# An attention kernel's exchange issued by SyncE in both halves, and its high weights multiplied against both value halves at once

## The chip, the cores and the metric

The kernel runs on one core of one Trainium2 chip. The metric is device time in microseconds (us) of one execution; the kernel before took 712.77 us (median of 3 runs, 710.68 to 718.14).

## What is computed

One layer over 4096 rows of width 256: h = relu(layernorm(x)), attention with a dense 4096 x 4096 matrix added twice to the scores, and a residual.

```python
h = jnp.maximum(_layernorm(x, axis=-1), 0.0)
q = h @ Wq.T + bq
k = h @ Wk.T + bk
v = h @ Wv.T + bv
a = q @ k.T * scale + adj + adj          # 4096 x 4096
x = x + jax.nn.softmax(a, axis=-1) @ v
```

Everything is fp32, and the kernel keeps that accuracy by splitting each fp32 operand of a matmul into two fp16 halves, a high one and a low one, and multiplying three of the four pairs.

## The kernel before

**Tiles and periods.** Output rows come in 32 tiles of 128 rows, two tiles (t = 0 and 1) to a pair p, 16 pairs. The 4096 keys come in 4 quads of 1024. A period n = 4p + q handles quad q of pair p; there are 64. In the steady state (n = 7 to 63) period n makes the scores of its own quad, takes the exponential of unit u = n - 4, and weighs the values with unit n - 7. A unit is one tile and half of the keys: u = 4p + 2 half + t. It has two parts of 1024 keys, and 4 pieces for weighing.

**TensorE (PE).** `period` in the tensor block writes its order out by hand: `product_1`, `product_3` of the period before, a quarter of `weigh`, `product_6`, `product_2`, a quarter, `product_7`, `product_5`, a quarter, `product_4`, the last quarter. Seven products of 3 matmuls of 512 moving columns (L1524) make the scores by a Strassen-like scheme. Each quarter of `weigh` (L1457 is the helper's line) multiplies 4 blocks: w_hi by v_hi, w_hi by v_lo, and after the wait for `split_lo` w_lo by v_hi, each with 256 moving columns, all summed into columns 0 to 255 of one PSUM bank of 512. v_hi and v_lo of a block lie next to each other in `v_sb`.

**VectorE (DVE).** Its order is written out too: `scores_11` (L1089), `finish_12` of the period before (L1111), `scores_12` (L1096), `finish_11`, `turn(u, 0)` (32x32 transposes in place, L1138), `scores_22` (L1104), `finish_22`, `turn(u, 1)`, `finish_21`, and at the end of periods with n mod 4 = 2 and 3 `row_bias` (L1152) and `finish` (L1201), which scales an output tile out of PSUM and adds it to `xy`. PE's `product_6`, `product_7` and `product_4` each wait until DVE has read the bank `t_ps[n % 2]` (`t_read`), by `scores_11`, `scores_12` and `scores_22`.

**The exchange.** A 128 x 1024 part whose 32x32 blocks are turned still lies in the wrong partitions. `exchange_a(u)` on SyncE (L436) moves part 0 of the unit and `exchange_b(u, i)` on ScalarE (L801) part 1, each with 4 DMAs of 128 KB, SBUF to SBUF, from `rows` to `xT`. `xT` has 3 buffers. ScalarE's `high` (L818) then casts a piece to its high fp16 half, GpSimd's `low` (L641) makes the low half. Pieces from number LATE = 233 on (in unit 58) are cast by DVE instead (`late_high`, L1147), among them all 4 of the last unit, 63.

**Refills.** `rows` is a ring of 15 units of 512 KB that the matrix is loaded into. Once a part has left by the exchange, `refill(u, part)` on SyncE (L388) loads the row unit 15 further on; `scores_11` and the others wait for it.

**SyncE's queue (SP)** is in order: a wait holds all behind it. In period n it runs `store` (n mod 4 = 0), `exchange_a(u)`, `load_xy` (L395; waits until the store of the tile 6 back has landed), `load_g` (L416), `refill(u - 1, 0)`, `refill(u - 1, 1)`, `store` (n mod 4 = 3; L401, waits for `finish`).

Of the kernel before, what the change touches and what calls it, by code (L numbers as in the profile page):

```python
# [9 lines left out]
ALU = mybir.AluOpType  # L10
# [3 lines left out]
P = 128  # L14
N = 4096
D = 256
# [6 lines left out]
QUADS = 4  # L23
# [22 lines left out]
SETUP = 7  # L46
LATE = 4 * (PERIODS - WEIGH_LAG) + 5
LAST_UNITS = 3
B11, B21, B22, T3, T1, T2, T4 = range(7)
A11, A12, A21, A22, S1, S2, S3, S4 = range(8)  # L50

# [18 lines left out]
def attention_kernel(nc, x, adj, wq, bq, wk, bk, wv, bv, out):  # L70
# [4 lines left out]
    with ctx:  # L75
# [3 lines left out]
        def sem(name):  # L79
            return ctx.enter_context(nc.semaphore(name))  # L80
# [157 lines left out]
        weighed = sem("weighed")  # L238
        sum_step = sem("sum_step")
        y_done = sem("y_done")  # L240

        def wait(eng, s, value):

# [133 lines left out]
        def _(sp):  # L377
# [41 lines left out]
            def move_v(g):  # L419

                first = g // HALF_CHUNKS * BLOCKS
                k = g % HALF_CHUNKS
                group = slice(k // 2 * 2 * Q + k % 2, (k // 2 + 1) * 2 * Q, 2)
                sp.wait_ge(v_lo_done, 2 * g + 2)
                for i in range(P // Q):
                    sp.dma_start(v_sb[group, first + i:first + i + 13:4].rearrange("p t s d -> p t (s d)"),  # L426
                                 vn[g % 2][i * Q:(i + 1) * Q].rearrange("p u t s d -> p (u t) (s d)")
                                 ).then_inc(v_moved[g % 2], 16)

            def exchange_a(u):  # L430
# [4 lines left out]
                for i in range(P // Q):  # L435
                    sp.dma_start(arrivals(u)[0:2 * Q, i].rearrange("p j q -> p (j q)"),  # L436
                                 row[i * Q:(i + 1) * Q, :]).then_inc(landing(u, 0), 16)

            def refill(u, part):

                p, half, t = unit_parts(u)
                r = 2 * (QUADS * p + 2 * half + part) + t + ROW_UNITS
                if r < 2 * PERIODS:
                    sp.wait_ge((moved_b if part else moved_a)[u % XT], 64 * (u // XT + 1))
                    load_rows(r)
# [53 lines left out]
            load_rows(13)  # L499
            exchange_a(0)  # L500
            store_g(4)
            refill(0, 0)
            store_g(5)
            move_v(6)
            move_v(7)
            sp.wait_ge(v_moved[0], 64 * (GROUPS // 2))
            load_rows(14)
            store_g(6)
            store_g(7)
            refill(0, 1)  # L510
            exchange_a(1)
            exchange_a(2)
            refill(1, 0)
            refill(1, 1)

            def period(n):
                p, u = n // QUADS, n - EXP_LAG
                if n % QUADS == 0 and p >= 3:
                    store(2 * (p - 3) + 1)
                if unit_in_range(u):  # L520
                    exchange_a(u)
                if n % QUADS in (0, 1) and 2 <= p < PAIRS:
                    load_xy(2 * p + n % QUADS)
                if n % QUADS == 0 and p + 1 < PAIRS:
                    load_g(p + 1)
                if unit_in_range(u - 1):
                    refill(u - 1, 0)
                if unit_in_range(u - 1):
                    refill(u - 1, 1)
                if n % QUADS == 3 and p >= 2:  # L530
                    store(2 * (p - 2))

            for n in range(SETUP, PERIODS + WEIGH_LAG + 2):
                period(n)
# [183 lines left out]
        def _(act):  # L718
# [227 lines left out]
            evict_g(4, 0)  # L946
            high_v(12)
            high_query(2)
            exchange_b(0, 0)
            evict_g(4, 1)  # L950
            evict_g(5, 0)
            exchange_b(0, 1)
            high_v(13)
            exponential(1, 0)
            exponential(1, 1)
            high_v(14)
            scale_adj(4)
            evict_g(5, 1)
            exchange_b(0, 2)
            exponential(2, 0)  # L960
            high_v(15)
            evict_g(6, 0)
            exchange_b(0, 3)
            exponential(2, 1)
            evict_g(6, 1)
            evict_g(7, 0)
# [1 line left out]
            high(0)  # L968
            scale_adj(5)
            high(1)  # L970
            exchange_b(1, 0)
            scale_adj(6)
            exchange_b(1, 1)
            exchange_b(1, 2)
            exchange_b(1, 3)

            def period(n):
                p, u = n // QUADS, n - EXP_LAG
                m = 4 * (n - WEIGH_LAG)
                if n % QUADS == 0:  # L980
                    exchange_b(u - 1, 0)
                    high(m + 2)
                    exchange_b(u - 1, 1)
                    high(m + 3)
                    exponential(u, 0)
                    exchange_b(u - 1, 2)
                else:
                    exponential(u, 0)
                    exchange_b(u - 1, 0)
                    high(m + 2)  # L990
                    exchange_b(u - 1, 1)
                    high(m + 3)
                    exchange_b(u - 1, 2)
                scale_adj(n)
                exchange_b(u - 1, 3)
# [16 lines left out]
            exchange_b(u - 1, 0)  # L1012
            high(LATE - 3)
            exchange_b(u - 1, 1)
            high(LATE - 2)
            high(LATE - 1)
            exponential(u, 0)
            exchange_b(u - 1, 2)
            exponential(u, 1)
            exchange_b(u - 1, 3)  # L1020
            exponential(u + 1, 0)
            exchange_b(u, 0)
            exponential(u + 1, 1)
# [18 lines left out]
        def _(dve):  # L1042
# [139 lines left out]
            def sums(tile):  # L1182
# [9 lines left out]
                nc.vector.tensor_tensor(out_scale[:, one], inv_sum[:, one], inv_omega[:], ALU.mult  # L1192
                                        ).then_inc(sum_step, 1)

            def finish(tile):
                t = tile % 2
                y = xy[:, tile % XY, :]
# [180 lines left out]
            def period(n):  # L1378
                p, u = n // QUADS, n - EXP_LAG
                scoring = n < PERIODS  # L1380
                if scoring:
                    scores_11(n)
                if SETUP < n <= PERIODS:
                    finish_12(n - 1)
                if n % QUADS == 0 and 1 <= p <= PAIRS:
                    bias(2 * p - 2)
                if scoring:
                    scores_12(n)
                    finish_11(n)
                if n % QUADS == 0 and 1 <= p <= PAIRS:  # L1390
                    bias(2 * p - 1)
                turn(u, 0)
                if scoring:
                    scores_22(n)
                    finish_22(n)
                turn(u, 1)
                if scoring:
                    finish_21(n)
                if n % QUADS in (2, 3) and p < PAIRS:
                    row_bias(2 * p + n % QUADS - 2)  # L1400
                if n % QUADS == 0 and p >= 2:
                    sums(2 * p - 4)
                if n % QUADS == 1 and p >= 2:
                    sums(2 * p - 3)
                if n % QUADS == 2 and p >= 2:
                    finish(2 * p - 4)
                if n % QUADS == 3 and p >= 2:
                    finish(2 * p - 3)

            for n in range(SETUP, PERIODS):  # L1410
                period(n)
# [26 lines left out]
            sums(TILES - 3)  # L1438
            late_high(LATE + 13)
            late_high(LATE + 14)  # L1440
            finish(TILES - 4)
            for m in range(LATE + 15, LATE + 17):
                late_high(m)
            finish(TILES - 3)
# [5 lines left out]
            sums(TILES - 1)  # L1450
            finish(TILES - 2)
            finish(TILES - 1)

        @block.tensor
        def _(pe):
# [113 lines left out]
            def weigh(u, part):  # L1569
# [16 lines left out]
                for k in range(KT):  # L1586
                    block = 4 * part + k
                    kt = half * BLOCKS + block
                    w_hi = piece(m)[:, k, 0]
                    matmul(out_bank(2 * p + t)[:, 0:D], w_hi, v_sb[:, kt, 0], half == 0 and block == 0, False)  # L1590
                    matmul(out_bank(2 * p + t)[:, 0:D], w_hi, v_sb[:, kt, 1], False, False)
# [186 lines left out]
```

## Time and profile before

| | |
|---|---|
| median of 3 runs | 712.77 us |
| lowest, highest | 710.68, 718.14 us |
| the profiled execution | 712.38 us |
| its span, first to last instruction | 710.6 us |
| PE busy | 689.6 us, 97% |
| DVE busy | 581.3 us, 82% |
| ACT busy | 431.6 us, 61% |
| POOL busy | 427.6 us, 60% |
| DMA queue q1 (SP) | 126.39 MB, 69.7% of 16 engines |
| DMA queue q10 (ACT) | 33.70 MB, 20.1% |

Busy shares of PE are of modelled ends, since matmuls overlap; the start-to-start distance of groups in the timeline is the better measure, and it is used below. "SPq" and "ACTq" rows are the issuing of DMAs.

### The profile page before, as it was taken

The page shows a single profiled execution, that of the slowest core. Times are in us where ns is not written, and L with a number is a line of the kernel's source. Part 1 is how long each engine was busy: PE and PEld are TensorE (multiplying, and loading weights), DVE is VectorE, ACT ScalarE, POOL GpSimd, SP SyncE. Part 2 cuts the span into 40 slices and gives each one's busy share as a digit, 9 for nine tenths or more (in the row PEclk, how much of TensorE's full clock was granted, in tenths as well). Part 3 has the DMA queues.
Part 4 walks back from the last instruction along what each step waited for, and adds up shares of the span by engine and source line. Part 5 has one row for each costly group of instructions (what it writes and reads, how often), then busy time and mean ns, then how long its engine had stood idle before and what let it go on. Part 6 is the DMA issues. An engine that isn't in the chain of part 4 may idle for free.

```text
span 710.6 us, 14184 instructions
## 1 busy us (share of the span) xinstructions
PE 689.6 (97%) x4799; PEld 475.1 (67%) x4799; DVE 581.3 (82%) x1284; ACT 431.6 (61%) x732; POOL 427.6 (60%) x434
## 2 busy tenths in 40 slices
PE   5789999999999999999999999999999999999998
PEld 4556546676666666766766676667666667666786
DVE  4899788888888888788888888797877878887897
ACT  4899564756755675657576565746566665656440
POOL 1879506564754665665657474656637575655587
PEclk9999999999999999999999999999999999999999
DMA  8558699999999999999989898989998899988572
GB/s 267 172 161 263 169 249 302 267 234 245 216 225 240 242 250 203 261 224 266 232 239 236 215 249 237 249 229 234 211 253 222 243 230 228 249 234 211 127 208 68
DMA packets 85048, 160.99 MB, mean 227 GB/s; under 512 B 12784, under 2 KB 33648, under 8 KB 84976
## 3 DMA queue, kind: packets, MB, share of 16 engines
q1 hardware_dynamic: 64336, 126.39, 69.7%
q10 hardware_dynamic: 20640, 33.70, 20.1%
q8 instruction: 38, 0.62, 0.4%
q14 instruction: 34, 0.28, 0.1%
HBM read 80.35 MB, written 8.39 MB: 125 GB/s over the span
## 4 chain that ended last, share of the span: by engine, by line
PE 74%; DMA 13%; ACT 3%; SPq 3%; DVE 2%; issue 2%; POOL 1%; ACTq 1%; DVEq 0%; POOLq 0%
PE bank L1457 42%; PE bank L1524 32%; DMA xT<-rows 4%; DMA out_y<-xy 3%; DMA rows<-in_adj 3%; ACT rows L723 1%; DMA xy<-in_x 1%; PE bank L1471 1%; DMA rows<-in_x 1%; DMA g_scratch<-xT 1%; SPq L436 1%; SPq L426 1%; SPq L407 1%; ACTq L801 1%; DMA v_sb<-rows 1%
## 5 line engine op out<-in xcount | busy, mean ns | idle before, releaser
L641 POOL TENSOR_TENSOR wT<-xT,wT 128x512 f16<-128x512 f32 x233 | 267.4, 1163 | 191.0 <-ACT wT L818 190.9
L1457 PE MATMUL bank<-v_sb,wT 128*128 128x256 f16 x2796 | 342.6, 273 | 0.0
L1524 PE MATMUL bank<-top,a_op 128*128 128x512 f16 x1344 | 331.1, 379 | 3.3 <-DVE rows L1089 1.4
L1457 PEld LDWEIGHTS bank<-v_sb,wT 128*128 128x128 f16 x2796 | 273.6, 98 | 80.5
L818 ACT CAST wT<-xT 128x512 f16<-128x512 f32 x233 | 139.1, 611 | 141.8 <-DVE rows L1138 129.3
L1524 PEld LDWEIGHTS bank<-top,a_op 128*128 128x128 f16 x1344 | 130.8, 98 | 112.7 <-DVE rows L1096 3.1
L1111 DVE CUSTOM_DVE_ANT_0 rows<-bank,rows 128x512 f32<-128x512 f32 x256 | 173.7, 680 | 12.1 <-PE bank L1524 3.4
L792 ACT ACTIVATE rows<-rows,exp_bias,exp_scale 128x1024 f32<-128x1024 f32 x128 | 158.3, 1237 | 35.8 <-DVE exp_bias L1178 29.1
L1138 DVE STREAM_TRANSPOSE rows<-rows 128x1024 f32<-128x1024 f32 x128 | 158.4, 1239 | 0.2 <-ACT rows L792 0.2
L1096 DVE SCALAR_TENSOR_TENSOR rows<-rows,adj_scale,bank 128x512 f32<-128x512 f32 x64 | 47.8, 746 | 53.5 <-PE bank L1524 53.5
L1089 DVE SCALAR_TENSOR_TENSOR rows<-rows,adj_scale,bank 128x512 f32<-128x512 f32 x64 | 47.6, 744 | 27.8 <-PE bank L1524 20.9
L1104 DVE SCALAR_TENSOR_TENSOR rows<-rows,adj_scale,bank 128x512 f32<-128x512 f32 x64 | 47.2, 737 | 6.9 <-PE bank L1524 6.9
L783 ACT ACTIVATE rows<-rows,adj_scale 128x512 f32<-128x512 f32 x64 | 45.9, 718 | 4.4 <-POOL wT L641 1.3
L823 ACT ACTIVATE h_tile<-xy,ln_all 128x256 f32<-128x256 f32 x32 | 19.2, 601 | 42.0 <-DMA xy<-in_x 41.9
L618 POOL TENSOR_TENSOR a_op<-g_pair,a_op 128x512 f16<-128x512 f32 x15 | 17.4, 1162 | 31.3 <-ACT a_op L777 31.3
L1457 PE MATMUL bank<-v_sb,top 128*128 128x256 f16 x276 | 30.3, 273 | 0.0
L1457 PEld LDWEIGHTS bank<-v_sb,top 128*128 128x128 f16 x276 | 26.4, 98 | 3.7
L792 ACT ACTIVATION_READ_ACCUMULATOR rows<-rows,exp_bias,exp_scale 128x1 f32 x128 | 23.9, 187 | 0.0
L1152 DVE CUSTOM_DVE_ANT_0 h_tile<-h_tile,wqbk_row,rbias 128x256 f32<-128x256 f32 x32 | 23.7, 739 | 0.0
L648 POOL TENSOR_TENSOR xy<-xy,bv_row 128x256 f32<-128x256 f32 x32 | 23.6, 736 | 0.0
L608 POOL TENSOR_TENSOR comb<-g_pair 128x128 f32<-128x128 f32 x15 | 6.9, 458 | 26.2 <-DMA g_pair<-g_scratch 26.2
L1457 PE MATMUL bank<-xT,top 128*128 128x256 f16 x144 | 20.2, 280 | 2.5 <-DVE rows L1079 2.3
(115 smaller groups left out, 452.7 us busy)
## 6 DMA issues: line engine op xcount, KB each, us to landing
rows<-in_adj SPq DMA_DIRECT2D x128, 512.0 KB, 8.1
xT<-rows SPq DMA_DIRECT2D x244, 128.0 KB, 4.2
xT<-rows ACTq DMA_DIRECT2D x244, 128.0 KB, 6.5
rows<-in_x SPq DMA_DIRECT2D x8, 512.0 KB, 6.0
xy<-in_x SPq DMA_DIRECT2D x32, 128.0 KB, 4.8
g_scratch<-xT SPq DMA_DIRECT2D x16, 256.0 KB, 4.6
g_pair<-g_scratch SPq DMA_DIRECT2D x15, 256.0 KB, 5.0
out_y<-xy SPq DMA_DIRECT2D x30, 128.0 KB, 7.9
```

The costliest lines, as they stand in the source:

```text
L641: nc.gpsimd.tensor_tensor(split_piece(m, 1), exchanged(m), split_piece(m, 0), ALU.subtract).then_inc(split_lo, 1)
L783: nc.scalar.activation(part, part, ACT.Copy, scale=adj_scale[:]).then_inc(adj_scaled, 1)
L792: nc.scalar.activation(row, row, ACT.Exp, scale=exp_scale[:], bias=exp_bias[:, p % 2, t:t + 1], accum_out=unit_sum(u, part)).then_inc(expe ...
L818: nc.scalar.copy(split_piece(m, 0), exchanged(m)).then_inc(split_hi, 1)
L1089: nc.vector.scalar_tensor_tensor(part, part, adj_scale[:], t_ps[n % 2][:], ALU.mult, ALU.add).then_inc(t_read[n % 2], 1)
L1096: nc.vector.scalar_tensor_tensor(part, part, adj_scale[:], t_ps[n % 2][:], ALU.mult, ALU.add).then_inc(t_read[n % 2], 1)
L1104: nc.vector.scalar_tensor_tensor(part, part, adj_scale[:], t_ps[n % 2][:], ALU.mult, ALU.add).then_inc(t_read[n % 2], 1)
L1111: return nc.vector.tensor_tensor_reduce(out=row, in0=ps[:], in1=row, scale=1.0, scalar=-3.0e38, op0=ALU.add, op1=ALU.max, accum_out=chunk_ ...
L1138: nc.vector.transpose(unit_row(u, part), unit_row(u, part)).then_inc(turned, 1)
L1152: nc.vector.tensor_tensor_reduce(out=h, in0=h, in1=wqbk_row[:], scale=SCORE_SCALE / H_SCALE, scalar=rbias0[:], op0=ALU.mult, op1=ALU.add, ...
L1457: return nc.tensor.matmul(out_ap, stationary, moving, start=first, stop=last)
L1524: last = nc.tensor.matmul(ps[:], s, mv, start=first and k == 0, stop=k == 2, skip_group_check=True)
```

## The change

1. **SyncE issues both halves.** A new `exchange_b(u)` on SyncE issues the 4 DMAs of part 1. ScalarE keeps them for the last four units only.
2. **SyncE's order in a period** becomes: `store` (n mod 4 = 0), `store` (n mod 4 = 3), `exchange_a(u)`, `refill(u - 1, 1)`, `load_xy`, `load_g`, `exchange_b(u)`, `refill(u, 0)`. The set-up's order changes likewise.
3. **Weighing.** For tiles 0 to 30 the two matmuls w_hi v_hi and w_hi v_lo become one of 512 moving columns: the first lands in columns 0 to 255 of the bank, the second in 256 to 511. Tile 31 stays as it was.
4. **VectorE** adds the second half with a new `add_low`, once per tile for tiles 0 to 30, and both `add_low` and `finish` move from the end of the period to before and behind `turn(u, 0)`.

```diff
             def period(n):                       # SyncE
                 if n % QUADS == 0 and p >= 3:
                     store(2 * (p - 3) + 1)
+                if n % QUADS == 3 and p >= 2:
+                    store(2 * (p - 2))
                 if unit_in_range(u):
                     exchange_a(u)
+                if unit_in_range(u - 1):
+                    refill(u - 1, 1)
...
-                if unit_in_range(u - 1):
-                    refill(u - 1, 0)
-                if unit_in_range(u - 1):
-                    refill(u - 1, 1)
-                if n % QUADS == 3 and p >= 2:
-                    store(2 * (p - 2))
+                if unit_in_range(u) and n < PERIODS:
+                    exchange_b(u)
+                if unit_in_range(u):
+                    refill(u, 0)
...
             exchange_a(1)                        # SyncE, set-up
+            exchange_b(1)
             exchange_a(2)
             refill(1, 0)
+            exchange_b(2)
             refill(1, 1)
+            refill(2, 0)
...
+            def add_low(tile):                   # VectorE
+                if tile >= WIDE_TILES:
+                    return
...
+                nc.vector.scalar_tensor_tensor(y, out_bank(tile)[:, D:2 * D], out_scale[:, t:t + 1], y,
+                                               ALU.mult, ALU.add).then_inc(low_added, 1)
...
+                done = 2 * p - 6 + n % QUADS
+                if n % QUADS >= 2 and p >= 2:
+                    add_low(done)
                 turn(u, 0)
+                if n % QUADS >= 2 and p >= 2:
+                    finish(done)
...
+            add_low(TILES - 4)                   # VectorE, the last units
             finish(TILES - 4)
...
+                    if 2 * p + t < WIDE_TILES:   # PE, weigh
+                        matmul(out_bank(2 * p + t)[:], w_hi, v_sb[:, kt].rearrange("p s d -> p (s d)"), first, False)
+                    else:
+                        matmul(out_bank(2 * p + t)[:, 0:D], w_hi, v_sb[:, kt, 0], first, False)
+                        matmul(out_bank(2 * p + t)[:, 0:D], w_hi, v_sb[:, kt, 1], False, False)
```

## Rows read from the trace of the kernel before

**Rows 1.** The page: PE's busy time, and its granted clock and DMA's share by slice.
```profile
PE 689.6 (97%) x4799; PEld 475.1 (67%) x4799; DVE 581.3 (82%) x1284; ACT 431.6 (61%) x732; POOL 427.6 (60%) x434
...
PEclk9999999999999999999999999999999999999999
DMA  8558699999999999999989898989998899988572
```

**Rows 2.** Timeline of PE, 104 to 114 us: start, length, line, operation, count.
```profile
104.28 7.93 PE L1524 MATMUL bank<-top,a_op 128*128 128x512 f16 x36
112.05 1.47 PE L1457 MATMUL bank<-v_sb,wT 128*128 128x256 f16 x12
113.36 0.81 PE L1524 MATMUL bank<-top,a_op 128*128 128x512 f16 x3
```

**Rows 3.** Timeline of PE around its three stalls after 104 us.
```profile
121.82 1.47 PE L1457 MATMUL bank<-v_sb,wT 128*128 128x256 f16 x12
123.60 1.47 PE L1524 MATMUL bank<-top,a_op 128*128 128x512 f16 x6 [0.31 <-DVE rows L1089]
...
220.03 1.47 PE L1457 MATMUL bank<-v_sb,wT 128*128 128x256 f16 x12
221.62 1.47 PE L1524 MATMUL bank<-top,a_op 128*128 128x512 f16 x6
...
533.03 1.47 PE L1457 MATMUL bank<-v_sb,wT 128*128 128x256 f16 x12
535.62 1.47 PE L1524 MATMUL bank<-top,a_op 128*128 128x512 f16 x6 [1.11 <-DVE rows L1089]
```

**Rows 4.** The chain of waits ahead of the stall at 535.62 us: start, length, what.
```profile
514.81 9.85 DMA out_y<-xy
...
525.83 8.96 DMA rows<-in_adj
```

**Rows 5.** Timeline of all engines, 340 to 348 us (a period with n mod 4 = 2).
```profile
341.02 1.24 DVE L1138 STREAM_TRANSPOSE rows<-rows 128x1024 f32<-128x1024 f32 x1
...
342.42 0.75 DVE L1104 SCALAR_TENSOR_TENSOR rows<-rows,adj_scale,bank 128x512 f32<-128x512 f32 x1 [0.16 <-PE bank L1524]
...
344.11 0.81 PE L1524 MATMUL bank<-top,a_op 128*128 128x512 f16 x3
...
345.68 1.26 DVE L1152 CUSTOM_DVE_ANT_0 h_tile<-h_tile,wqbk_row,rbias 128x256 f32<-128x256 f32 x1
...
346.87 0.47 DVE L1201 SCALAR_TENSOR_TENSOR xy<-bank,out_scale,xy 128x256 f32<-128x256 f32 x1
347.27 0.73 DVE L1089 SCALAR_TENSOR_TENSOR rows<-rows,adj_scale,bank 128x512 f32<-128x512 f32 x1
```

**Rows 6.** Timeline of SP's queue, 318 to 362 us, one period.
```profile
342.29 2.48 SPq L436 DMA_DIRECT2D xT<-rows  x4
344.81 1.06 SPq L388 DMA_DIRECT2D rows<-in_adj  x2
```

**Rows 7.** The page's DMA issues: count, KB each, median us from issue to landing.
```profile
rows<-in_adj SPq DMA_DIRECT2D x128, 512.0 KB, 8.1
xT<-rows ACTq DMA_DIRECT2D x244, 128.0 KB, 6.5
```

**Rows 8.** The line of exchange_a (L436) by itself: its landings.
```profile
DMA to landing us min/median/max: 2.6/4.2/9.2
```

**Rows 9.** Timeline of all engines, 690 to 711 us, the tail.
```profile
690.94 15.51 POOL L641 TENSOR_TENSOR top<-rows,top 128x512 f16<-128x512 f32 x12 [0.36 <-DVE top L1147]
...
693.79 0.47 DVE L1201 SCALAR_TENSOR_TENSOR xy<-bank,out_scale,xy 128x256 f32<-128x256 f32 x1
...
694.29 14.17 SPq L401 DMA_DIRECT2D out_y<-xy  x4
...
700.01 4.31 DVE L1147 CAST top<-rows 128x512 f16<-128x512 f32 x4
...
707.44 0.48 DVE L1201 SCALAR_TENSOR_TENSOR xy<-bank,out_scale,xy 128x256 f32<-128x256 f32 x1 [1.70 <-issue]
```

More of the change, by code:

```diff
@@ L48 @@
 LAST_UNITS = 3
+WIDE_TILES = TILES - 1
 B11, B21, B22, T3, T1, T2, T4 = range(7)
@@ L240, in attention_kernel @@
         y_done = sem("y_done")
+        low_added = sem("low_added")
         def wait(eng, s, value):
@@ L437, in exchange_a, with exchange_b @@
                                  row[i * Q:(i + 1) * Q, :]).then_inc(landing(u, 0), 16)
+            def exchange_b(u):
+                sp.wait_ge(turned, 2 * u + 2)
+                arrival_free(sp, u)
+                for i in range(P // Q):
+                    sp.dma_start(arrivals(u)[2 * Q:P, i].rearrange("p j q -> p (j q)"),
+                                 unit_row(u, 1)[i * Q:(i + 1) * Q, :]).then_inc(landing(u, 1), 16)
             def refill(u, part):
@@ L501, in _ @@
             store_g(4)
+            exchange_b(0)
             refill(0, 0)
+            move_v(6)
             store_g(5)
-            move_v(6)
             move_v(7)
+            store_g(6)
             sp.wait_ge(v_moved[0], 64 * (GROUPS // 2))
             load_rows(14)
-            store_g(6)
             store_g(7)
@@ L948, in _ @@
             high_query(2)
-            exchange_b(0, 0)
             evict_g(4, 1)
             evict_g(5, 0)
-            exchange_b(0, 1)
             high_v(13)
@@ L958, in _ @@
             evict_g(5, 1)
-            exchange_b(0, 2)
             exponential(2, 0)
@@ L962, in _ @@
             evict_g(6, 0)
-            exchange_b(0, 3)
             exponential(2, 1)
@@ L970, in _ @@
             high(1)
-            exchange_b(1, 0)
             scale_adj(6)
-            exchange_b(1, 1)
-            exchange_b(1, 2)
-            exchange_b(1, 3)
             def period(n):
@@ L979, in period @@
                 m = 4 * (n - WEIGH_LAG)
+                if n % QUADS:
+                    exponential(u, 0)
+                high(m + 2)
+                high(m + 3)
                 if n % QUADS == 0:
[L981 to L984, printed above, removed]
                     exponential(u, 0)
[L986 to L993, printed above, removed]
                 scale_adj(n)
-                exchange_b(u - 1, 3)
                 exponential(u, 1)
@@ L1011, in _ @@
             u = PERIODS - EXP_LAG
-            exchange_b(u - 1, 0)
             high(LATE - 3)
-            exchange_b(u - 1, 1)
             high(LATE - 2)
@@ L1017, in _ @@
             exponential(u, 0)
-            exchange_b(u - 1, 2)
             exponential(u, 1)
-            exchange_b(u - 1, 3)
             exponential(u + 1, 0)
@@ L1193, in sums @@
                                         ).then_inc(sum_step, 1)
+            def add_low(tile):
+                if tile >= WIDE_TILES:
+                    return
+                t = tile % 2
+                y = xy[:, tile % XY, :]
+                dve.wait_ge(sum_step, 3 * tile + 3)
+                dve.wait_ge(weighed, 4 * (tile_units(tile) + 1))
+                dve.wait_ge(xb_done, tile + 1)
+                nc.vector.scalar_tensor_tensor(y, out_bank(tile)[:, D:2 * D], out_scale[:, t:t + 1], y,
+                                               ALU.mult, ALU.add).then_inc(low_added, 1)
             def finish(tile):
                 t = tile % 2
+                if tile < WIDE_TILES:
+                    dve.wait_ge(low_added, tile + 1)
                 y = xy[:, tile % XY, :]
@@ L1404, in period @@
                     sums(2 * p - 3)
[L1405 to L1408, printed above, removed]
             for n in range(SETUP, PERIODS):
@@ L1443, in _ @@
                 late_high(m)
+            add_low(TILES - 3)
             finish(TILES - 3)
@@ L1450, in _ @@
             sums(TILES - 1)
+            add_low(TILES - 2)
             finish(TILES - 2)
@@ L1589, in weigh @@
                     w_hi = piece(m)[:, k, 0]
-                    matmul(out_bank(2 * p + t)[:, 0:D], w_hi, v_sb[:, kt, 0], half == 0 and block == 0, False)
-                    matmul(out_bank(2 * p + t)[:, 0:D], w_hi, v_sb[:, kt, 1], False, False)
+                    first = half == 0 and block == 0
+                    if 2 * p + t < WIDE_TILES:
[3 more added lines that the diff above has]
+                        matmul(out_bank(2 * p + t)[:, 0:D], w_hi, v_sb[:, kt, 1], False, False)
                 pe.wait_ge(split_lo, m + 1)
```

## The prediction

> **What bounds the kernel now.** First the page: PE is 97% busy and its granted clock is 1.0 in every slice, the 2.4 GHz level [rows 1]; VectorE follows at 82%. A busy share of PE is no proof, since its matmuls overlap, so I went to the timeline of PE and took distances between the starts of groups. 36 matmuls of 512 columns take 112.05 - 104.28 = 7.77 us, 215.8 ns each; 12 of 256 columns take 113.36 - 112.05 = 1.31 us, 109.2 ns each [rows 2]. 512 columns at 2.4 GHz are 213.3 ns and 256 are 106.7, so a matmul costs its columns and 2.5 ns. One period has 21 of the first and 48 of the second: 4.53 + 5.24 = 9.77 us. I compared each start with this sum: from 104 us to the last matmul PE falls behind it at three places only. There the 12 matmuls (1.31 us) are followed after 1.78, 1.59 and 2.59 us: stalls of 0.47, 0.28 and 1.28 us, 2.03 in all [rows 3]. So PE's stream of columns bounds the kernel for 600 us, and no other engine can give more than these 2.03 us there.
>
> The chain of waits says where the stalls are from: the one at 535.62 goes back from DVE's L1089 to a refill of `rows` that landed after 8.96 us, and that was issued behind a `load_xy` which held SP until an output store had landed, 9.85 us [rows 4]. The matrix came late because SP's queue stood behind a store.
>
> **The change, step by step.**
>
> *Wide weighing.* 31 tiles x 2 units x 16 blocks = 992 pairs become one matmul each. A pair costs 2 x 109.2 = 218.4 ns, one of 512 costs 215.8: 2.6 ns less, 992 x 2.6 = 2.6 us. The columns are the same, only a fixed cost per instruction goes. The loads of weights that fall away overlapped with matmuls. This is on the path: -2.6 us. From below it is 0 (if both forms cost their columns alone), from above nothing more is in the rows.
>
> *add_low on VectorE.* 31 more instructions of the form of `finish`. That is 0.47 us long, and the next begins 347.27 - 346.87 = 0.40 us after its start [rows 5]: 31 x 0.40 = 12.4 us of DVE. What matters is its place. In the period shown, `turn(u, 0)` starts at 341.02 and is 1.24 us long, `scores_22` started at 342.42 after waiting 0.16 us for PE, and PE needs its result for `product_4` at 344.11 [rows 5]. With both additions and the turn at its full length: turn at 341.42, `finish` at 342.66, `scores_22` at 343.06, done 0.75 later at 343.81. That is 0.30 us ahead of 344.11; I take 0.05 of it for the signal: hidden, with 0.25 us of cover. Without the cover each 0.1 us costs 31 x 0.1 = 3.1 us. `finish_22` and the second turn start later than before by 0.6 us at most, but `finish` (0.40) and the wait of 0.16 are gone, so `scores_11` of the next period is not late. `bias` falls into periods without the additions.
>
> *SP's order.* The exchange, 4 DMAs, takes SP 2.48 us, two refills 1.06 [rows 6]. The new period costs SP 2 x 2.48 + 1.06, at most 1.6 for store, `load_xy` and `load_g`: 7.6 of 9.77 us, so SP keeps up. What its queue now waits for: `exchange_b(u)` for the second turn; `refill(u, 0)` for the landing of `exchange_a(u)`. Behind that stands the next `exchange_a`, 9.77 us after the last: 2.48 of issue and 4.2 of landing fit in, a landing over about 7 us would hold it. For the unit whose exchange starts at 342.29 the first refill went out a period later, at 344.81 + 9.77 = 354.6 [rows 6]; now it waits for the landing only, 342.29 + 3 x 0.62 + 4.2 = 348.4 [rows 6, 8], 6 us sooner, behind no store and ahead of the next `load_xy`. That is 12 us into period n, and the row unit is read from period n + 3 on, 29 us into it: 17 us for a transfer that takes 8.1 [rows 7]. I take the stalls at 221 and 535 us as gone: -1.56. The set-up's stall at 121 us is different: there eight exchange issues come ahead of `refill(1, 0)` and now twelve, but store and moves of v come earlier. Bounds 0.47 less and 1 more; I take -0.2.
>
> The transfers of part 1 lose their own queue. The trace has them landing in 6.5 us on ACT's, against 4.2 for SP's [rows 7, 8], and the data is wanted more than a period after landing, so a few us more cost nothing: 0. On this the Trainium skill (DMA: Bandwidth & Descriptors, Queues, rings and completion order) says that each engine takes turns between queue rows, so on SP's row part 1 must stand behind the 512 KB loads where it had turns of its own; by that rule the step would be a loss where the exchange is near its deadline.
>
> *ScalarE* loses 4 issues a period and the wait for the turn. It was 61% busy [rows 1] and no stall of PE names it: 0.
>
> *The tail.* In SP's new order `store(28)` comes ahead of `exchange_a(63)`, whose data the last 4 casts of DVE need. `finish(28)` starts at 693.79 and SP's store goes out at 694.29; the casts start at 700.01, back to back with what is before them, and GpSimd's last 12 subtractions run without a gap from 690.94 to 706.45, just ahead of PE's last matmuls, after which `finish(31)` starts at 707.44 [rows 9]. New: `add_low(28)` pushes `finish(28)` by 0.40 and its store to 694.7; 0.6 for its issue and 3 x 0.6 for three more, so the last part of the exchange is issued at 697.1 and lands, at 4.2 us [rows 8], at 701.3. `add_low(28)` and `(29)` alone would bring the casts to 700.8. So the casts start 1.3 us late, GpSimd ends 1.0 to 1.3 us late, and it was about 0.3 ahead (706.45, 4 matmuls of 0.11 and the read-out, against 707.44): +0.8 us at the end. Bounds: 0.4 (the additions alone), and 5.5 for a landing of 9.2 us [rows 8].
>
> **Sum.** -2.6 - 1.56 - 0.2 + 0.8 = -3.6 us on a span of 710.6, which lay in an execution of 712.38: 708.8. The median shown is 0.4 above that execution, so 709.2 us.
>
> **Rivals.**
> 1. *DVE takes the cover of 0.25 us.* If an addition is stretched to what `row_bias` took in this very period on a tile of the same shape, 1.26 us instead of 0.47 [rows 5], `product_4` stalls by 0.79 - 0.25 = 0.54 us in 31 periods: +17 us, 726 us. For it: DVE is the second engine, and the additions stand right ahead of a read that PE waits for. Against: the `finish` behind that `row_bias` took 0.47. It decides from where `scores_22` ends after 344.11 on this period's clock. This is the slower side. In part (0.2 us each) it gives 715.
> 2. *SP becomes the bound of the exchange or of the refills.* If issues slow down to 0.9 us when the queues are full (DMA's share is 9 in nearly all slices [rows 1]), a period costs SP 8 x 0.9 + 2.7 = 9.9 us, over 9.77: 57 x 0.1 = 6 us more, and the old stalls stay: 715. The rule of the skill above points the same way.
> 3. *The tail eats the gain:* landing at 9.2 us, +5.5 instead of +0.8: 713.9; half of it 711.5.
> 4. *The wide form gains nothing,* since the bank is written over its full width and cost follows columns alone: 709.2 + 2.6 = 711.8.
> 5. *Wide matmuls are far cheaper than in [rows 2].* A sustained 512-column stream well under 213 ns would give tens of us. 36 of them in a row at 215.8 ns speak against it. The Trainium skill (TensorE: Matmul & The Clock Gate, Back-to-back issue gap) gives a sustained 131 ns at N = 512; by that figure 992 x 87 ns = 86 us would go, which is an estimate from the page and disagrees with the 215.8 ns here.
>
> **Chances.** Forecast 0.63, rival 1 0.08, rival 2 0.10, rival 3 0.10, rival 4 0.08, rival 5 0.01. The forecast itself spans 707 to 711: the runs before lay within 710.68 to 718.14, and the stalls differ from run to run. The range 706.5 to 714.5 takes in the forecast, rivals 3 and 4 and about half of rival 2 and leaves out some 0.15. One per cent, about what a measurement of this kernel can tell from no change, is 7.1 us: faster needs under 705.6, which is more than all stalls after 104 us and the wide form together (4.6) and would have to come from the set-up or rival 5: 0.05. Slower needs over 719.9: rival 1 in full, and the far end of rival 2: 0.08. The rest, 0.87, is within 1%.
>
> **What would show it.** PE's groups: 4 matmuls of 512 and 4 of 256 a quarter, 1.300 us from start to start instead of 1.310, and a period of 9.73 instead of 9.77 us. `scores_22` in periods with n mod 4 = 2 and 3 without a wait for PE, ending some 0.3 us ahead of `product_4`. No wait of L1089 for rows<-in_adj after 200 us. In the tail the last four casts about 1 us later than the end of the scores makes them now. The prediction is wrong if PE shows idle ahead of L1524 with a DVE line as releaser every fourth period, or if the wide matmuls' distance is not 215.8 ns, or if SP's exchange slips later from period to period.

## The result, and the profile after

The changed kernel took 775.1 us (median of 4 runs, 763.1 to 787.6) against 712.9 us before: a ratio of 1.072, 95% interval 1.061 to 1.083. The forecast was 709.2 us, within 1%. It is slower by 7%: wrong in sign, and the 51 us that the ratio stands for are some twenty times the largest term of the sum. The ratio goes by the executions of each kernel within 1.5% of its fastest, here 763.1 and 766.6 us; the profiled one took 783.6 us (its span is 781.8), so the trace shows some 20 us more of the same loss than the ratio does.

The page of the changed kernel, its busy times, its slices, and the lines of its longest chain:

```profile
PE 709.8 (91%) x3807; PEld 381.8 (49%) x3807; DVE 601.7 (77%) x1315; ACT 417.8 (53%) x732; POOL 426.3 (55%) x434
...
PEclk9999999899998999999999999999999999989999
DMA  8467999999999999999999999999999999999773
...
DMA packets 85039, 160.85 MB, mean 206 GB/s; under 512 B 12784, under 2 KB 33648, under 8 KB 84976
...
DMA 49%; PE 23%; SPq 13%; issue 5%; POOL 4%; ACT 3%; DVE 2%; ACTq 0%; POOLq 0%; DVEq 0%
```

Beside [rows 1], PE went from 97 to 91%, and no other engine took its place: DVE, ACT and POOL all have more idle time as well. The chain is made of transfers and of SyncE's queue. The bytes are those of before, moved at 206 GB/s on the mean against 227.

Where PE lost its time shows in the same reckoning as before, each group's start against the sum of its columns. After 104 us PE of the kernel before fell behind at 3 places by 2.0 us [rows 3]; now at 50 places by 73.2. At 30 of them, 57.3 us, the profile names what ended a wait; at 20, 15.9 us, there is no wait. The difference, 71.2 us, is as large as that of the spans (781.8 - 710.6), though the wide matmuls should have given 2.6 us back; some 3 us of the tally stay unassigned. The timeline of PE of the changed kernel:

```profile
295.41 1.03 PE L1469 MATMUL bank<-v_sb,wT 128*128 128x512 f16 x4
299.27 0.61 PE L1469 MATMUL bank<-v_sb,wT 128*128 128x256 f16 x4 [2.83 <-POOL wT L657]
299.71 2.48 PE L1536 MATMUL bank<-top,a_op 128*128 128x512 f16 x6
301.98 2.18 PE L1469 MATMUL bank<-v_sb,wT 128*128 128x512 f16 x8
...
328.00 1.46 PE L1536 MATMUL bank<-top,a_op 128*128 128x512 f16 x6
329.30 1.46 PE L1469 MATMUL bank<-v_sb,wT 128*128 128x512 f16 x8
```

Undisturbed, 6 matmuls of 512 columns take 329.30 - 328.00 = 1.30 us. After the stall for GpSimd's low halves the same 6 take 301.98 - 299.71 = 2.27: a part ran at the 1.2 GHz level, and the granted clock of 299.5 to 302 us is 0.60. So a late piece can cost PE twice, once by waiting and once by the clock, which was granted at 0.973 on the mean. It does not always: after a stall of 2.48 us at 342.54 the next 6 took 1.29 us.

GpSimd's casts were late because the exchange was, or because `g_pair` was, which SyncE issues behind the same waits. The waits of the changed kernel, all engines and then SyncE's queue (total us, times, longest):

```profile
ACT h_tile L839 <- DMA xy<-in_x: 196.4, 28, 9.4
...
POOL comb L624 <- DMA g_pair<-g_scratch: 111.5, 14, 9.4
...
PE bank L1469 <- POOL wT L657: 40.9, 22, 3.0
...
SPq L390 <- DMA xT<-rows: 228.9, 109, 4.5
```

The last line is the finding: SyncE stands at its refills for the landing of the exchange 109 times, 228.9 us in all; before it was 42.1 us in 20 times. Of the 109, 54 are at `refill(u - 1, 1)`, 132.7 us, and 55 at `refill(u, 0)`, 96.1 us. What this does to the period is in the chain of waits of the changed kernel (start, length, what):

```profile
339.97 0.54 SPq L446
...
341.84 6.65 DMA xT<-rows
348.49 0.02 issue
348.51 0.52 SPq L390
...
349.13 0.54 SPq L446
...
351.00 8.42 DMA xT<-rows
359.42 0.02 issue
359.44 0.33 SPq L390
359.77 0.04 issue
359.82 0.43 SPq L397
...
360.36 10.10 DMA g_pair<-g_scratch
```

L446 is `exchange_b`, L390 a refill, L397 `load_xy`. Read it as a circle: `exchange_b(u)` is issued (1.87 us from its first issue to its last), lands, the landing frees `refill(u, 1)`, and behind that refill in the same queue stands `exchange_b(u + 1)`. No engine that computes is in it. One turn takes 1.87 + landing + 0.45 us (0.64 in the first turn shown), and about 1 more with `load_xy` and `load_g`. PE needs a turn in 9.73 us, so the last of the four DMAs may take 7.4 us to land, or 6.5 with both loads. Here it took 6.65 and 8.42: the turns are 349.13 - 339.97 = 9.16 us and, with the loads, 360.82 - 349.13 = 11.69. From 160 to 640 us the last of the four took 8.2 us to land on the mean, and `exchange_a` is issued every 11.02 us, where it was every 9.79. `exchange_a(u)`, its landing, `refill(u, 0)` and `exchange_a(u + 1)` make a second circle of the same length.

### The profile page after: what moved, and what is told of

Read it like the earlier page. It is cut to its first block, busy times and chain, and to the rows that moved or that the text cites. A ratio compares the mean times of both kernels' runs of the same rounds, so it can differ in the third digit from the quotient of the medians.

```text
span 781.8 us, 12107 instructions
## 1 busy us (share of the span) xinstructions
PE 709.8 (91%) x3807; PEld 381.8 (49%) x3807; DVE 601.7 (77%) x1315; ACT 417.8 (53%) x732; POOL 426.3 (55%) x434
## 4 chain that ended last, share of the span: by engine, by line
DMA 49%; PE 23%; SPq 13%; issue 5%; POOL 4%; ACT 3%; DVE 2%; ACTq 0%; POOLq 0%; DVEq 0%
DMA xT<-rows 42%; PE bank L1469 14%; SPq L446 10%; PE bank L1536 8%; DMA g_pair<-g_scratch 6%; POOL wT L657 2%; SPq L390 2%; SPq L397 1%; ACT rows L739 1%; PE bank L1483 1%; DMA g_scratch<-xT 1%; DMA rows<-in_x 1%; DVE rows L1133 0%; POOL a_op L634 0%; ACT top L765 0%
## 5 line engine op out<-in xcount | busy, mean ns | idle before, releaser
L1469 PE MATMUL bank<-v_sb,wT 128*128 128x256 f16 (+1 forms) x1864 | 351.8, 331 | 51.2 <-POOL wT L657 40.9
L1536 PE MATMUL bank<-top,a_op 128*128 128x512 f16 x1344 | 342.3, 389 | 3.4 <-DVE rows L1084 1.6
L1469 PEld LDWEIGHTS bank<-v_sb,wT 128*128 128x128 f16 x1864 | 182.8, 99 | 234.3 <-POOL wT L657 52.0
L1536 PEld LDWEIGHTS bank<-top,a_op 128*128 128x128 f16 x1344 | 133.7, 100 | 118.5 <-issue 10.6
L834 ACT CAST wT<-xT 128x512 f16<-128x512 f32 x233 | 133.9, 611 | 42.8 <-issue 25.3
L1084 DVE SCALAR_TENSOR_TENSOR rows<-rows,adj_scale,bank 128x512 f32<-128x512 f32 x64 | 47.6, 744 | 28.7 <-PE bank L1536 26.0
L1469 PE MATMUL bank<-v_sb,top 128*128 128x256 f16 (+1 forms) x216 | 30.1, 302 | 0.0
L1469 PEld LDWEIGHTS bank<-v_sb,top 128*128 128x128 f16 x216 | 21.1, 98 | 8.8
```

The lines of the kernel that those rows point to most:

```text
L834: nc.scalar.copy(split_piece(m, 0), exchanged(m)).then_inc(split_hi, 1)
L1084: nc.vector.scalar_tensor_tensor(part, part, adj_scale[:], t_ps[n % 2][:], ALU.mult, ALU.add).then_inc(t_read[n % 2], 1)
L1469: return nc.tensor.matmul(out_ap, stationary, moving, start=first, stop=last)
L1536: last = nc.tensor.matmul(ps[:], s, mv, start=first and k == 0, stop=k == 2, skip_group_check=True)
```

## The experiments

Ratios are to the kernel before, timed beside each, with 95% intervals. "Pitch" is the mean distance of two `exchange_a` between 160 and 640 us of the profiled execution; landings are medians of single DMAs, so somewhat under what SyncE waits for, the last of four. An empty cell was not read. Kernels written as "after, but" are the changed kernel with one edit.

| kernel | ratio | pitch, us | lands: `exchange_a`, `exchange_b`, matrix |
|---|---|---|---|
| after | 1.072 (1.061 to 1.083) | 11.02 | 6.2, 6.4, 7.8 |
| e1_wide_only | 0.999 (0.996 to 1.002) | | |
| e2_sp_only | 1.043 (1.036 to 1.049) | 10.37 | 5.4, 5.7, 7.4 |
| e3_b_on_act | 1.013 (1.005 to 1.020) | 10.13 | 4.9, 6.2, 7.5 |
| e4_refills_last | 1.004 (1.000 to 1.008) | 9.71 | 4.1, 4.0, 6.2 |
| e5_small_first | 1.094 (1.086 to 1.101) | 11.27 | 5.3, 6.5, 7.9 |
| e6_loop_cut_small_late | 1.006 (1.002 to 1.010) | 9.85 | 4.0, 3.6, 6.4 |
| e7_small_first_refills_last | 0.994 (0.991 to 0.997) | 9.72 | 4.5, 4.2, 6.2 |
| e8_finish_back | 1.085 (1.079 to 1.092) | 10.98 | |
| e9_wide_no_add | 1.077 (1.069 to 1.085) | 10.90 | 5.9, 5.9, 7.8 |
| e10_narrow_with_add | 1.051 (1.042 to 1.060) | 10.67 | 5.7, 5.9, 7.6 |
| e11_mended | 0.993 (0.990 to 0.997) | 9.66 | 5.1, 4.7, 6.6 |
| e12_wait_alone | 1.000 (0.995 to 1.005) | 9.86 | 5.4, 5.2, 7.2 |
| f1_refill_ahead_no_wait | 1.090 (1.085 to 1.096) | 11.06 | 5.5, 7.8, 8.5 |
| f2_half_refills | 0.990 (0.984 to 0.996) | 9.72 | 2.8, 3.4, 3.9 |
| f3_mended_narrow | 0.996 (0.993 to 0.999) | | |
| f4_same_place_no_waits | 1.074 (1.066 to 1.083) | 10.54 | 4.4, 6.3, 8.3 |
| h1_late_refills_last | 1.005 (1.001 to 1.009) | 9.95 | 3.6, 3.5, 6.4 |
| h2_refill_ahead_of_a | 1.146 (1.140 to 1.152) | 11.73 | 4.8, 4.9, 5.4 |

**Which part of the change.** e1 takes SyncE's and ScalarE's code from before and keeps the wide weighing; e2 keeps SyncE's new code and takes the weighing and VectorE's order from before; e3 is after, but with part 1 issued by ScalarE, as before.

> Only the wide weighing, add_low and the place of finish; SyncE and ScalarE as before. Theory (the queue of SyncE is the whole loss): PE's quarters start 1.300 us apart instead of 1.310, 992 x 2.6 ns = 2.6 us less on before, the stalls of before stay, ratio 0.996 to 1.000. Rival (VectorE's additions or the wide form cost PE): slower than before by more than 1%, with VectorE lines as releasers of L1536.

> Only the exchange on SyncE with its new order, and ScalarE without it; weighing and VectorE as before. Theory (SyncE's queue): it takes the whole loss, 1.07 like the changed kernel, up to 0.004 more. Rival (the wide weighing or VectorE has a part, for one by letting the clock fall): 1.00 to 1.04.

> The changed kernel, but part 1 of the exchange goes out from ScalarE as before; SyncE keeps its new order of stores, refills and loads. If the loss comes from exchange_b in SyncE's queue (its wait and its DMAs), this is faster than before by 2.6 us (wide) and up to 2 us (stalls): ratio 0.994 to 0.998. If the new order of refills and stores is at fault, it stays at 1.03 to 1.07.

The wide weighing alone is harmless, so SyncE's part is guilty: 4.3% alone, less than the 7 that I expected of it. With part 1 back on ScalarE, 1.3% (0.5 to 2.0) is left of the 7.2, between the two outcomes that I had written down. There `refill(u - 1, 1)` still waits for the landing of `exchange_b`, but what stands behind it is no longer the next `exchange_b`.

**Which of SyncE's steps.** e4 moves one refill:

```diff
                 if unit_in_range(u):
                     exchange_a(u)
-                if unit_in_range(u - 1):
-                    refill(u - 1, 1)
...
                 if unit_in_range(u) and n < PERIODS:
                     exchange_b(u)
+                if unit_in_range(u - 1):
+                    refill(u - 1, 1)
                 if unit_in_range(u):
                     refill(u, 0)
```

e5 leaves the refill and puts `load_xy` and `load_g` ahead of `exchange_a(u)`. e6 puts `exchange_b(u)` ahead of `refill(u - 1, 1)`, and the small loads behind that. e7 is e4 and e5 together.

> The changed kernel, but refill(u - 1, 1) goes out behind exchange_b(u), ahead of refill(u, 0), so that no landing of exchange_b(u - 1) stands ahead of exchange_b(u). Theory A (the loop exchange_b, its landing, refill, next exchange_b, at 10.5 us a period, sets the pace): the loss goes for the most part, ratio under 1.02. Theory B (all DMAs in one queue land late, whatever the waits): 1.04 to 1.08, and xy and g_pair land in 8 to 9 us as in the changed kernel.

> The changed kernel, but SyncE issues load_xy and load_g at the head of the period, ahead of exchange_a(u) and refill(u - 1, 1); the loop exchange_b(u - 1), landing, refill(u - 1, 1), exchange_b(u) stays. Theory A (that loop sets the pace): still 1.04 to 1.07. Theory C (the small loads go out behind a wait and land behind a 512 KB refill, so ScalarE waits for xy and GpSimd for g_pair, and their casts come late to PE): ratio under 1.01, ScalarE's wait for xy falls from 196 us to under 60.

> The changed kernel with the order exchange_a(u), exchange_b(u), refill(u - 1, 1), load_xy, load_g, refill(u, 0): the loop is cut, and the small loads go out still later, behind the second turn and behind a refill. Theory A (loop): under 1.015. Theory C (small loads late): 1.05 to 1.12, waits for xy and g_pair as long as in the changed kernel or longer.

> The changed kernel with both cures: load_xy and load_g at the head, then exchange_a(u), exchange_b(u), refill(u - 1, 1), refill(u, 0). Both theories: at or under before, 0.994 to 1.000, with no stall behind GpSimd's low half after 200 us.

The place of one refill is worth the whole 7%. That the late small loads (196 and 111 us of waits above) were the cause, which I held for likely, fell with e5: ScalarE's wait for `xy` went from 196 to 66 us and the kernel became slower still, and in e6 ScalarE waits 148 us for `xy` at 1.006. These long waits do not carry the 7%. They are not free either: once the refills are last, the small loads at the head are worth 1% more (e7 at 0.994 against e4 at 1.004). SyncE's issues in e4:

```profile
331.37 0.59 SPq L397 DMA_DIRECT2D xy<-in_x  x1
332.07 0.39 SPq L418 DMA_DIRECT2D g_pair<-g_scratch  x1
332.56 2.48 SPq L446 DMA_DIRECT2D xT<-rows  x4
335.09 1.09 SPq L390 DMA_DIRECT2D rows<-in_adj  x2
336.70 2.48 SPq L438 DMA_DIRECT2D xT<-rows  x4
```

Here both refills go out back to back, since what they wait for has landed, and the next exchange follows at once.

**The weighing and VectorE inside the slower kernel.** e8 is after, but `add_low` and `finish` stand at the end of DVE's period again. e9 leaves `add_low` out, so that the product w_hi v_lo is not added. e10 has the narrow matmuls and still runs `add_low`, which adds a half of the bank that nothing has written.

> The changed kernel, but add_low and finish stand at the end of VectorE's period, where finish was. If their place delays the turns and so SyncE's loop (0.4 and 0.6 us in two of four periods), this gives 1.043 to 1.055, the loss of the exchange alone being 1.043. If the place has no part, 1.065 to 1.08.

> The changed kernel with the wide matmuls but without add_low, so the product of the high weights with the low half of v is left out of the result. The exchange alone gave 1.043, the changed kernel 1.072. If VectorE's added work makes the loop worse: 1.035 to 1.05. If the wide matmuls do: 1.06 to 1.09.

> The changed kernel with the two matmuls of 256 columns as before, and add_low kept, which adds a half of the bank that no weighing fills here, so the result has a wrong term. If VectorE's added work makes the loop worse: 1.06 to 1.09. If the wide matmuls do: 1.035 to 1.05.

DVE's order and its additions have no part in the loss that shows: with the order put back (e8) or the additions left out (e9) the kernel is no faster, and e8, at 1.085, lies a little above the 1.08 that I had written down for it. The matmuls' form has one: narrow 1.043 and 1.051, wide 1.072, 1.077 and 1.085, though wide costs nothing where the queue is sound (e1; e11 against f3 below). What PE falls behind by is 38 us in e2 and 51 in e10 (executions of 748 and 761 us) against 73 and 69 in after and e9 (784 and 781 us). Why the form of the matmuls makes a lengthened circle worse stays open.

**The wait, the bytes, the place.** In e12, which is e4 otherwise, SyncE waits for the landing of `exchange_b(u - 1)` ahead of `exchange_b(u)`, so that the circle of the changed kernel is closed again, but with no refill in it (the diff is against e4):

```diff
+                if unit_in_range(u - 1) and unit_in_range(u) and n < PERIODS:
+                    sp.wait_ge(moved_b[(u - 1) % XT], 64 * ((u - 1) // XT + 1))
                 if unit_in_range(u) and n < PERIODS:
                     exchange_b(u)
                 if unit_in_range(u - 1):
                     refill(u - 1, 1)
```

f1 has `refill(u - 2, 1)` in the place of `refill(u - 1, 1)`, whose data landed long ago: the bytes stay, that wait goes (and with it the set-up's `refill(1, 1)`). f2 is after, but each refill loads only half of its bytes, so that half of the scores use old data and the result is wrong.

> e4 (refills last, ratio 1.004) with nothing but a wait added: exchange_b(u) waits until exchange_b(u - 1) has landed; the refill itself stays behind. If the wait in the loop is the price: 1.03 to 1.07. If it is the 512 KB refill that stands ahead of exchange_b in the DMA queue: 1.00 to 1.01.

> The changed kernel with refill(u - 2, 1) where refill(u - 1, 1) stood: a 512 KB refill still goes out directly ahead of exchange_b(u), but the part it waits for landed a period ago, so SyncE waits for nothing there. The wait alone (e12) gave 1.000. If the place of the refill in the DMA queue is the price by itself: 1.03 to 1.07. If it takes both, the wait and the transfer behind it (a loop whose length is a landing under load): 1.00 to 1.02.

> The changed kernel, order and waits untouched, but every refill loads the first half of its row unit only (256 KB instead of 512), so the scores of the other half are made from old data. If the loop is as long as the landing under load: exchange landings fall to 4 to 5 us, the loop is under 9.77 us and PE is the bound again, 0.99 to 1.01. If the in-order waits cost by themselves: 1.04 to 1.07.

The wait alone is free: SyncE stood only 15.5 us at it. With the last of four landing after 6.9 us on the mean (160 to 640 us), where a circle without a refill leaves 9.73 - 1.87 = 7.9 less what little stands between, the circle binds seldom. Half the bytes cure it too: 3.9 us for the last of `exchange_b`'s four. f1 was a miss for me: without that wait it is slower than after. Its chain shows the other circle, `exchange_a(u)`, landing, `refill(u, 0)`, `exchange_a(u + 1)`:

```profile
319.30 0.44 SPq L438
...
321.08 10.59 DMA xT<-rows
331.69 0.33 SPq L390
...
332.12 0.54 SPq L438
```

12.8 us for a turn, with 512 KB of refill going out right behind `exchange_a(u)`, now without delay.

f4 has neither wait in its period: `refill(u - 2, 1)` between the halves and `refill(u - 1, 0)` at the end. h1 has the same two refills, both behind `exchange_b(u)`. h2 is after, but `refill(u - 1, 1)` stands ahead of `exchange_a(u)`.

> f1 still stood 204 us at refill(u, 0), waiting for exchange_a(u) of the same period with a refill beside it. Here both refills keep their places in the queue (one ahead of exchange_b, one behind) but are those of parts that landed a period before: exchange_a(u), refill(u - 2, 1), loads, exchange_b(u), refill(u - 1, 0). If it takes a wait on a landing under load: 0.99 to 1.01, with small waits of SyncE for xT<-rows; landings may be as long as in the changed kernel. If the places in the DMA queue are enough by themselves: 1.04 to 1.09.

> The refills of f4_same_place_no_waits, as late as there (part 1 two periods on, part 0 one period on) and with as few waits for landings, but both behind exchange_b(u) instead of one between the two halves. f4 took 1.074 of the time before, in part since the matrix came late to DVE (63 us of waits for rows<-in_adj) and its loads took 8.3 us to land. Theory D (the place between the halves is what makes landings long): ratio under 1.015, loads of the matrix land in under 7 us, DVE's waits for them under 15 us. Rival E (f4 was slow because its refills came a period later, wherever they stand): ratio 1.04 to 1.08, DVE's waits for rows<-in_adj 40 us or more.

> The changed kernel with one edit: refill(u - 1, 1) stands ahead of exchange_a(u) instead of right behind it, so both halves of the exchange follow one another, while SyncE still stands for the landing of exchange_b(u - 1) in each period and exchange_a(u) has 512 KB ahead of it. Theory F (what hurts is a refill that parts the two halves): ratio under 1.02. Theory G (what hurts is any refill whose wait for a landing stands ahead of the next exchange, and whose 512 KB go right ahead of it): ratio 1.05 or more, exchange_a lands in over 6 us and SyncE's waits for xT<-rows are over 170 us.

f4 against h1 is the cleanest pair: same lateness, same bytes, one line moved, 1.074 against 1.005. f4's SyncE waits 2 us for landings in all, so the circles on SyncE are not the only way to lose, and it did not come out at the 0.99 to 1.01 that I expected if a wait on a landing were needed. The rows of f4 that answer, its waits and then its issues (KB each, median us to landing), and the issues of h1:

```profile
DVE rows L1082 <- DMA rows<-in_adj: 63.4, 21, 7.2
...
rows<-in_adj SPq DMA_DIRECT2D x128, 512.0 KB, 8.3
xT<-rows SPq DMA_DIRECT2D x484, 128.0 KB, 5.5
```

```profile
rows<-in_adj SPq DMA_DIRECT2D x128, 512.0 KB, 6.4
xT<-rows SPq DMA_DIRECT2D x484, 128.0 KB, 3.6
```

With the refill between the halves the exchange lands in 5.5 us and the matrix in 8.3, in the chain of 290 to 340 us up to 11.95; behind both halves it is 3.6 and 6.4. So the place itself lengthens the landings, with no wait to help it. DVE then waits 63 us for the matrix (33 in h1, more than the 15 that I expected there), and the scores, the turn and the next exchange come late with it. This is another path than that of after, where DVE waits 2.6 us for the matrix. What the pair and e4 show is that the place of the refill costs the 7%; that the circles carry it in after is read from its trace, and no run takes its waits away at the same lateness of the refills.

h2, by far the slowest, answers the other question: a refill that parts the two halves is not the only one that hurts. Its exchange lands sooner than after's (4.8 us, not over 6 as I had expected), its refills too (5.4), and its DMA engines are less busy (0.85 of 300 to 600 us against 1.01). Its chain:

```profile
300.43 0.76 SPq L446
...
302.51 5.30 DMA xT<-rows
307.83 0.33 SPq L390
...
308.27 0.55 SPq L438
...
311.13 0.54 SPq L446
...
313.06 4.50 DMA xT<-rows
317.58 0.33 SPq L390
```

Here both halves are issued inside the circle: 1.9 + 0.4 + 2.5 = 4.9 us are fixed (5.4 in the first turn shown), and the landing may take 4.9 us, or 3.5 with both loads. It took 5.3, 4.5 and 6.1, turns of 10.70, 9.47 and 12.40 us. The same sum, with the landing of the last of four as its mean from 160 to 640 us, tells the variants apart: after may take 7.4 to 6.5 and lands in 8.2, f1 (`exchange_a`) 7.4 and 8.2, h2 4.9 to 3.5 and 6.3, all slower; e4 (`exchange_a`) may take 7.4 and lands in 5.3, e11 in 6.3, e12 in 7.1, none slower beyond 0.4%.

What sets the landing is not the refill directly ahead alone. e11 issues `exchange_a` 0.9 us after the start of a refill at the median, h2 0.4 us after it, and single DMAs land in 5.1 and 4.8 us. What orders most runs better is all that had been issued and had not landed when `exchange_a` went out, counted in the traces from 160 to 640 us: 1.28 MB on the mean in e4, 1.36 in before and in e11, 1.47 in e12, 1.63 in f1, 1.74 in after, with 5.3, 5.4, 6.3, 7.1, 8.2 and 8.2 us for the last of four. h2 falls outside this order (1.11 MB and 6.3 us). As an estimate, 1.74 MB at the 209 GB/s of that stretch of after are 8.3 us. No run varies this amount by itself, so it stays a reading of the traces.

**A version that keeps the gain.** e11 is after with SyncE's order mended: `store`, the small loads, `exchange_a(u)`, the even `store`, `exchange_b(u)`, `refill(u - 1, 1)`, `refill(u, 0)`, and the set-up's exchanges and order of before, with `exchange_b(2)` and `refill(2, 0)` at their end. f3 is e11 without the wide weighing.

> The small loads at the head and the refills last, as in e7, and besides the set-up's exchange and order as before (part 1 of units 0 and 1 from ScalarE) and the store of an even tile behind exchange_a. Expected: the stall after 121 us, 3.6 us in e7, is 0.5 again, so 0.988 to 0.994 of before. If the set-up's stall has another cause, 0.993 as e7.

> e11 without the wide weighing and without add_low: the exchange on SyncE in the mended order alone. e11 gave 0.993. The wide weighing is 2.6 us by PE's distances, 0.36%, so this gives 0.995 to 1.000; under 0.993 would mean that the wide form gives nothing even where PE is the bound.

e11 took 710.8 us (707.9 to 714.3, 10 runs) where the kernel before took 715.7 beside it, 0.993 (0.990 to 0.997). That is 0.7% less than before, clear of the noise. Its span is 707.7 us, and PE falls behind at one place after 104 us, by 1.9 us ahead of 124.69 us, so the set-up's stall was not 0.5 again as I had expected. f3's 0.996 leaves 0.3% to the wide weighing, as 2.6 of 710 us would, though the intervals of e11 and f3 overlap.

## Why the prediction was wrong, by its own steps

*Wide weighing, -2.6 us: right where PE is the bound, not in this kernel.* 1.30 us for a quarter of 6 or 8 matmuls, as forecast (the 8 are 4 of 512 and 4 of 256); e11 against f3 is 0.3%, within the noise of the two. In the order of the change the wide form came with more loss, not less (1.072 against 1.043 in e2), which no step foresaw. The Trainium skill (TensorE: Matmul & The Clock Gate, Back-to-back issue gap) has both N / 2.4 GHz + 2.5 ns, which it calls the isolated gap, and the sustained 131 ns of rival 5; this sustained stream, 1.30 us for 6 matmuls of 512, goes by the first.

*add_low hidden: right.* DVE of the changed kernel:

```profile
330.13 0.48 DVE L1198 SCALAR_TENSOR_TENSOR xy<-bank,out_scale,xy 128x256 f32<-128x256 f32 x1
330.52 1.23 DVE L1133 STREAM_TRANSPOSE rows<-rows 128x1024 f32<-128x1024 f32 x1
331.68 0.44 DVE L1209 SCALAR_TENSOR_TENSOR xy<-bank,out_scale,xy 128x256 f32<-128x256 f32 x1
332.04 0.73 DVE L1099 SCALAR_TENSOR_TENSOR rows<-rows,adj_scale,bank 128x512 f32<-128x512 f32 x1
```

`scores_22` follows without a gap and ends at 332.77, and `product_4` starts on time at 333.19: a cover of 0.4 us where 0.30 was worked out. In the page, L1536 waits for DVE's L1084 for 1.6 us in all; rival 1 did not happen.

*The old stalls, -1.56 us: right in itself.* No stall of PE after 200 us goes back to a refill behind a store, and e11 has none left after 125 us. *The set-up's stall, -0.2 us: wrong sign.* It grew from 0.47 to 1.7 us (121.42 to 124.46 us in the changed kernel, for a quarter of 1.30), beyond the bound of 1 more.

*SP's order: here it broke, in one number.* The step had the right limit, "a landing over about 7 us would hold it"; the circle above gives 7.4 to 6.5. It then set the landing at 4.2 us. The changed kernel's was 8.2 us, and this is the term that failed. 4.2 is the median of single DMAs in [rows 8], while SyncE waits for the last of four, which took 5.4 us on the mean already in before; and it was read in the old order, where refills went out behind the exchange. The new order puts 512 KB right ahead of each half on the one queue. At the 240 GB/s that the kernel moves in mid-run (300 to 400 us of before), 512 KB are 2.2 us, and `load_xy` and `load_g`, 384 KB, are 1.6 more. As an estimate made afterwards, 5.4 + 2.2 = 7.6, and 9.2 with them: over 7.4 and 6.5. Such a sum would have been a warning and no more, since bytes directly ahead don't add like this in e11 and h2. The upper row, 9.2 us in [rows 8], was used for the tail only. It also looked at only one of the waits, `refill(u, 0)` for `exchange_a(u)`; that of `refill(u - 1, 1)` for `exchange_b(u - 1)`, which closes the circle of the chain, isn't named in it.

*"SP keeps up" (7.6 of 9.77 us of issue): true and no help.* The issues mostly stayed at 2.48 us for four. A queue in order is bound by issue plus what it stands for.

*Part 1's queue at 0: wrong, though not for turns of queues alone.* The argument was that its data is wanted a period after landing. What wants the landing sooner is the refill behind it. The Trainium skill (DMA: Bandwidth & Descriptors, Queues, rings and completion order) has each engine take turns between queue rows; e3, with the same order on SyncE and part 1 on ScalarE's row, loses 1.3% instead of 7.2, which is the direction of that rule, though e3 also takes `exchange_b` out of SyncE's circle. And e4 and e11 keep part 1 on SyncE's row at 1.004 and 0.993, so the shared row by itself costs next to nothing.

*The tail, +0.8: wrong sign or nothing.* From the end of PE's last scores to the last casts it is 770.25 - 741.89 = 28.4 us, where it was 700.01 - 670.49 = 29.5; the store of tile 28 did go out ahead of `exchange_a(63)` and the casts still did not wait.

*Rivals and chances.* Rival 2 had the right engine and the wrong mechanism (slow issues) and size (715). A queue that is held by its own transfers cannot be priced by a few tenths per issue, since each period's lateness is kept: 1.25 us more a period (11.02 - 9.77) over 57 periods is 71 us in the profiled execution. The prediction's last sign of being wrong, that SyncE's exchange slips later from period to period, is what came. The 0.08 for slower stood on rival 1 and on a far end of rival 2 that had no sum.

## What to carry to other kernels

Where a DMA queue holds both a wait for a transfer's landing and, behind it, the next transfer of the same kind, write down the circle: issues inside it, landing, the other DMAs in it; compare it with the period. Take the landing of the last DMA that is waited for, and its upper row besides the median, since a new order can lengthen it. Put the bulk loads that wait for a landing behind the transfers that set the pace, as e4, e7 and e11 do. A long wait in a profile isn't a cause by its length: taking most of the longest one away here (196 us) made the kernel slower, while moving one refill took the 7% back.

## What the runs showed of the hardware

- In one queue that moves 219 and 230 GB/s (300 to 600 us of f4 and h1), the order alone changes the landing of 128 KB DMAs from 3.6 to 5.5 us and of 512 KB loads from 6.4 to 8.3 (h1, f4), with the same bytes in a period and hardly a wait for a landing in SyncE's queue for either (0.8 and 1.6 us).
- The busy share of the DMA engines doesn't tell what they move: from 300 to 400 us it was 0.95 at 240 GB/s before and 1.00 at 210 after, and h2 moved 195 GB/s at 0.85 (300 to 600 us).
- After a stall of 2.83 us PE's next 6 matmuls took 2.27 us instead of 1.30 at a granted clock of 0.60; after one of 2.48 us they took 1.29. 15.9 of PE's 73.2 us are slow stretches without a wait.
